# Weights of the first norm as one row, spread by a product with ones; new order of the first transfers; dt of batch 0 in four tiles

## The reference

```python
h = rmsnorm(hidden_states, ln1_w)            # x * rsqrt(mean(x*x) + eps) * ln1_w
zxbcdt = h @ w_in.T                          # 512 -> 512 + 768 + 4 columns
z, xs, Bs, Cs, dt = jnp.split(zxbcdt, ...)
xBC = silu(conv(concat([xs, Bs, Cs])) + conv_b)
dt = softplus(dt + dt_bias); A = -exp(A_log)
... # chunked scan over 4 chunks of 128 positions, gate with silu(z), @ w_out.T
```

## Time and profile before

| | |
|---|---|
| median of 3 runs | 495.55 us (494.87 to 496.28) |
| the profiled execution | 494.94 us, its span 493.2 us |
| TensorE busy | 473.5 us, 96% of the span |
| VectorE, ScalarE, GpSimd busy | 316.8, 236.8, 215.1 us |
| mean granted clock of TensorE | 0.994 |
| TensorE's share of the chain that ended last | 80% |

### The profile page before, as it was taken

How to read it: one execution, slowest core, us unless ns; L and a number is a source line. 1 busy time by engine, 2 the same in 40 slices (tenths; PEclk the granted TensorE clock), 3 DMA queues, 4 the chain that set the end, 5 groups by cost and what they waited for, 6 DMA issues and landing times.

```text
span 493.2 us, 6223 instructions
## 1 busy us (share of the span) xinstructions
PE 473.5 (96%) x2104; PEld 377.1 (76%) x2104; DVE 316.8 (64%) x518; ACT 236.8 (48%) x444; POOL 215.1 (44%) x242
## 2 busy tenths in 40 slices
PE   8998999988999989999999899999999999999995
PEld 7886677765767768888788778888888888888884
DVE  3793587746688856677998889865957523411223
ACT  5887667766556666455343245234805430033300
POOL 5835476526773596767877000010004442133321
PEclk9998999999999999999999999999999999999998
DMA  7531022003212415342332166410300000200001
GB/s 247 200 110 49 38 86 65 21 23 102 75 59 86 167 45 193 130 171 86 130 105 83 69 214 213 170 45 7 122 21 1 0 0 1 85 2 0 2 15 70
DMA packets 14431, 40.80 MB, mean 83 GB/s; under 512 B 2368, under 2 KB 2368, under 8 KB 14400
## 3 DMA queue, kind: packets, MB, share of 16 engines
q1 hardware_dynamic: 14400, 40.41, 24.1%
HBM read 38.30 MB, written 2.10 MB: 82 GB/s over the span
## 4 chain that ended last, share of the span: by engine, by line
PE 80%; DVE 11%; issue 4%; ACT 3%; POOL 2%; POOLq 0%; DVEq 0%
PE psA L1621 8%; PE psA L1622 8%; PE psA L1410 6%; PE psA L1412 6%; PE psB L1631 4%; PE psB L1630 4%; PE psA L1416 3%; PE psA L1418 3%; PE psA L1600 3%; PE psA L1599 3%; PE psA L1596 3%; DVE xbc L1168 3%; PE psB L1596 2%; PE psB L1600 2%; PE psB L1599 2%
## 5 line engine op out<-in xcount | busy, mean ns | idle before, releaser
L1621 PE MATMUL psA<-xT_h,q_gu 128*128 128x512 f32 x176 | 70.1, 398 | 0.0
L1622 PE MATMUL psA<-xT_l,q_gu 128*128 128x512 f32 x176 | 69.1, 393 | 0.0
L669 POOL TENSOR_SCALAR var<-mv 128x1 f32<-128x1 f32 x16 | 4.9, 305 | 128.7 <-DVE mv L1060 128.6
L1031 ACT ACTIVATE gate_t<-psA 128x512 f32<-128x512 f32 x22 | 13.2, 598 | 75.1 <-PE psA L1622 75.1
L816 POOL TENSOR_TENSOR int_l<-prod_t,int_h 128x512 fp32r<-128x512 f32 x22 | 28.7, 1306 | 45.7 <-ACT int_h L1036 45.7
L1362 DVE TENSOR_TENSOR prod_t<-gate_t,psA 128x512 f32<-128x512 f32 x22 | 15.1, 689 | 51.7 <-PE psA L1622 48.6
L727 POOL TENSOR_TENSOR beta<-wsum,beta 128x512 fp32r<-128x512 f32 x28 | 36.1, 1312 | 24.8 <-ACT beta L892 24.8
L1621 PEld LDWEIGHTS psA<-xT_h,q_gu 128*128 128x128 f32 x176 | 33.1, 188 | 8.2
L1622 PEld LDWEIGHTS psA<-xT_l,q_gu 128*128 128x128 f32 x176 | 33.1, 188 | 7.4
L1631 PE MATMUL psB<-q_dn,int_l 128*128 128x512 f32 x88 | 34.3, 389 | 0.0
L1630 PE MATMUL psB<-q_dn,int_h 128*128 128x512 f32 x88 | 34.2, 389 | 0.0
(11 more groups left out here) (251 smaller groups left out, 1358.8 us busy)
## 6 DMA issues: line engine op xcount, KB each, us to landing
raw<-in_f_gu_t SPq DMA_DIRECT2D x22, 512.0 KB, 3.3
raw<-in_w_gu_t SPq DMA_DIRECT2D x14, 512.0 KB, 3.8
raw<-in_f_dn_t SPq DMA_DIRECT2D x10, 512.0 KB, 3.6
raw<-in_w_gu_t SPq DMA_DIRECT2D x14, 256.0 KB, 2.9
raw<-in_w_dn_t SPq DMA_DIRECT2D x7, 512.0 KB, 3.3
raw<-in_w_in_t SPq DMA_DIRECT2D x5, 512.0 KB, 4.4
x<-in_hidden SPq DMA_DIRECT2D x8, 256.0 KB, 4.9
out<-x SPq DMA_DIRECT2D x8, 256.0 KB, 2.0
```

The costliest lines, as they stand in the source:

```text
L1621: nc.tensor.matmul(ps, w, seq(xT_h, k, b), start=k == 0, stop=False)
L1622: done = nc.tensor.matmul(ps, w, seq(xT_l, k, b), start=False, stop=k == KD - 1)
```

## The change

The weights of the first norm come as one row of 512 (2 KB) and not as 128 copies (256 KB). A product of a row of ones with this row spreads them over the 128 partitions of a bank of `psA`, and VectorE copies them to `ln1_sb`. TensorE's thirty transposes of the identity become 8 ahead of this product and 18 behind it. On SyncE's queue the row goes first, the four tiles of batch 0 follow, the weights of dt have a semaphore of their own, and the first input weights go ahead of five small constants. dt of batch 0 is made for one tile of 128 positions at a time, and `aneg` moves on ScalarE from `prepare` to behind the copy of dt.

```diff
-    steps += [("norm1", t) for t in range(NC)]
+    steps += [("ln1rows",)] + [("norm1", t) for t in range(NC)]
     steps += [("turn1", 0), ("turn1", 1), ("prepare",), ("turn1", 2), ("turn1", 3), load("in", 0)]
+    steps += [("dtpart", c) for c in range(NC - 1)]
     steps += [("norm1", 4), ("norm1", 5), ("dt", 0), load("in", 1), ("norm1", 6), ("norm1", 7)]
...
-WARM_UP = 30
+WARM_FIRST, WARM_UP = 8, 18
 KEEP_WARM = {1: 11, 2: 8, 3: 9}
...
-            load_x(0)
-            load_x(1)
-            sp.dma_start(ln1_sb[:], ln1_w.to_broadcast([P, D])).then_inc(ln1_loaded, 16)
-            for t in range(2, NC):
+            sp.dma_start(ln1_row[:], ln1_w).then_inc(ln1_loaded, 16)
+            for t in range(NC):
                 load_x(t)
-
-            sp.dma_start(wdt_raw[:], w_dt).then_inc(consts_loaded, 16)
+            sp.dma_start(wdt_raw[:], w_dt).then_inc(wdt_loaded, 16)
+            load_weights(0)
             sp.dma_start(alog_sb[:], a_log.to_broadcast([P, H])).then_inc(consts_loaded, 16)
...
+            nc.gpsimd.memset(one_row[:], 1.0)
...
-                s.wait_ge(consts_loaded, N_CONST)
+                s.wait_ge(wdt_loaded, 16)
                 s.wait_ge(wdt_ready, 1)
                 nc.scalar.activation(wdt[:, :, 0:H], wdt_raw[:], ACT.Copy).then_inc(wdt_ready, 1)
-                nc.scalar.activation(aneg[:], alog_sb[:], ACT.Exp).then_inc(aexp_ready, 1)
...
+                    if b == 0:
+                        s.wait_ge(consts_loaded, N_CONST)
+                        nc.scalar.activation(aneg[:], alog_sb[:], ACT.Exp).then_inc(aexp_ready, 1)
...
+                if kind == "ln1rows":
+                    v.wait_ge(*done_a(step))
+                    nc.vector.tensor_copy(ln1_sb[:], bank_a(step)).then_inc(freed_a(step)[0], 1)
+                elif kind == "norm1":
...
                     if t == 0:
-                        v.wait_ge(ln1_loaded, 16)
+                        v.wait_ge(*freed_a(("ln1rows",)))
...
+            def part_of_dt(c):
+
+                pe.wait_ge(xTh_ready, TURNS.index(("turn1", c)) + 1)
+                pe.wait_ge(wdt_ready, 3)
+                ps = open_a(("dt", 0)) if c == 0 else bank_a(("dt", 0))
+                for k in range(KD):
+                    nc.tensor.matmul(ps[:, chunk(c)], wdt[:, k, :], xT_h[:, k, chunk(c)], start=c == 0 and k == 0,
+                                     stop=False)
+                pe.wait_ge(*freed_b(("turn1", c)))
+                for k in range(KD):
+                    done = nc.tensor.matmul(ps[:, chunk(c)], wdt[:, k, :], xT_l[:, k, chunk(c)], start=False,
+                                            stop=c == NC - 1 and k == KD - 1)
+                return done
+
+            keep_warm(WARM_FIRST)
...
+                if kind == "ln1rows":
+
+                    pe.wait_ge(ln1_loaded, 16)
+                    nc.tensor.matmul(open_a(step), one_row[:], ln1_row[:], start=True, stop=True).then_inc(a_done, 1)
+                    keep_warm(WARM_UP)
+                elif kind == "dtpart":
+                    part_of_dt(at[0])
...
+                elif step == ("dt", 0):
+                    part_of_dt(NC - 1).then_inc(a_done, 1)
```

More of the change, by code:

```diff
@@ L270, in psum_jobs @@
         kind, at = s[0], s[1:]
-        if kind == "dt":
-            a.append(("dt", *at))
+        if kind == "ln1rows" or kind == "dt" and at[0] == 1:
+            a.append(s)
+        elif kind == "dtpart" and at[0] == 0:
+            a.append(("dt", 0))
         elif kind == "inproj":
@@ L374, in layer_kernel @@
             ("t_f", 134912, [P, 4, 2, P], F32), ("ln2_sb", 140032, [P, D], F32), ("nrm2", 142080, [P, D], F32))
-        xn, ln1_sb, wdt = overlay(("xn", 61440, [P, NT, D], F32), ("ln1_sb", 77824, [P, D], F32),
-                                  ("wdt", 79872, [P, KD, P], F32R))
+        xn, ln1_sb, wdt, ln1_row, one_row = overlay(("xn", 61440, [P, NT, D], F32), ("ln1_sb", 77824, [P, D], F32),
+                                           ("wdt", 79872, [P, KD, P], F32R), ("ln1_row", 81920, [1, D], F32),
+                                           ("one_row", 83968, [1, P], F32))
         tT_h, tT_l, alpha, act, beta, a22, wsum, u_t, v_t, c12, q8 = overlay(
@@ L402, in layer_kernel @@
         ln2_loaded = sem("ln2_loaded")
+        wdt_loaded = sem("wdt_loaded")
         consts_loaded = sem("consts_loaded")
@@ L583, in layer_kernel @@
         NORMS = [s for s in SCHEDULE if s[0] in ("norm1", "outproj", "ln1", "ln2")]
-        N_CONST = 16 * 6
+        N_CONST = 16 * 5
         def norm_number(step):
@@ L625, in _, with load_weights @@
             sources = {"in": w_in, "out": w_out, "ga": w_gu, "gb": w_gu, "dn": w_dn, "sumgu": f_gu, "qgu": f_gu, "sumdn": f_dn, "qdn": f_dn}
-            load_x(0)
-            load_x(1)
-            sp.dma_start(ln1_sb[:], ln1_w.to_broadcast([P, D])).then_inc(ln1_loaded, 16)
-            for t in range(2, NC):
+            def load_weights(n):
+                kind, *at = LOADS[n]
+                src = sources[kind][at[0]]
+                wide = down_width(at[0]) if kind in ("sumdn", "qdn") else KD * P if kind == "ga" else RAW
+                sp.dma_start(raw[:, n % RAW_SLOTS, 0:wide], src[:, 0:wide]).then_inc(raw_loaded[n % RAW_SLOTS], 16)
+            sp.dma_start(ln1_row[:], ln1_w).then_inc(ln1_loaded, 16)
+            for t in range(NC):
                 load_x(t)
-            sp.dma_start(wdt_raw[:], w_dt).then_inc(consts_loaded, 16)
+            sp.dma_start(wdt_raw[:], w_dt).then_inc(wdt_loaded, 16)
+            load_weights(0)
             sp.dma_start(alog_sb[:], a_log.to_broadcast([P, H])).then_inc(consts_loaded, 16)
@@ L637, in _ @@
             sp.dma_start(convb_sb[:], conv_b).then_inc(consts_loaded, 16)
-            for n, (kind, *at) in enumerate(LOADS):
+            for n in range(len(LOADS)):
                 if n >= RAW_SLOTS:
@@ L642, in _ @@
                         sp.wait_ge(*used)
-                src = sources[kind][at[0]]
-                wide = down_width(at[0]) if kind in ("sumdn", "qdn") else KD * P if kind == "ga" else RAW
-                sp.dma_start(raw[:, n % RAW_SLOTS, 0:wide], src[:, 0:wide]).then_inc(raw_loaded[n % RAW_SLOTS], 16)
+                if n >= 1:
+                    load_weights(n)
                 if n == 1:
@@ L689, in prepare @@
             def prepare():
-                pool.wait_ge(consts_loaded, N_CONST)
+                pool.wait_ge(wdt_loaded, 16)
                 pool.wait_ge(wdt_ready, 2)
@@ L695, in prepare @@
                     .then_inc(wdt_ready, 1)
+                pool.wait_ge(consts_loaded, N_CONST)
                 nc.gpsimd.tensor_tensor(heads(diag_d[:]), ident[:].unsqueeze(1).to_broadcast([P, H, P]),
@@ L1063, in _ @@
                 kind, at = step[0], step[1:]
-                if kind == "norm1":
+                if kind == "ln1rows":
+                    v.wait_ge(*done_a(step))
+                    nc.vector.tensor_copy(ln1_sb[:], bank_a(step)).then_inc(freed_a(step)[0], 1)
+                elif kind == "norm1":
                     t = at[0]
@@ L1446, in keep_warm @@
                     nc.tensor.transpose(psA[:, 3, 0:P], ident[:], ident[:])
-            keep_warm(WARM_UP)
+            def part_of_dt(c):
[11 more added lines that the diff above has]
+            keep_warm(WARM_FIRST)
             for step in SCHEDULE:
                 kind, at = step[0], step[1:]
-                if kind == "turn1":
+                if kind == "ln1rows":
[4 more added lines that the diff above has]
+                    part_of_dt(at[0])
+                elif kind == "turn1":
                     pe.wait_ge(nrm_ready, at[0] + 1)
```

## The result

The changed kernel takes **498.43 us** (median of 4 runs, 497.74 to 498.88); the kernel before, beside it on the same chip, 495.21 us (494.73 to 496.28). The ratio is 1.006, with an interval from 1.0046 to 1.0075: about 3 us slower, near the forecast of 498.5. The profiled execution took 497.74 us.

The account below looks back on a forecast made before the run. Past the start TensorE bounds the kernel; the first 45 us hang on dt, norms, VectorE's convolutions and ScalarE. 0.44 + 7.10 + 0.15 - 2.32 - 0.7 - 1.7 = +3.0, giving 498.5 us; range 494.8 to 500.4, the forecast's own 497.6 to 500.4.

Parts of the forecast that it names:

- That is 0.44 us later than 7.31: TensorE's start: eight fillers, the product with ones and 18 fillers end at 7.75, so the first tile's transpose starts 0.44 later.
- The remark under the rivals: TensorE's start: a clock rise one or two us later, from the one-row product, would add up to 1 us.
- I take 0.222: dt in four tiles: each of 32 narrow fp32r products costs 0.222 us, 7.10 in all.
- rival 2: dt: not slower, a narrow product costs one pass, 0.111; 495.0 with the clock held, 496.6 without; chance 0.31.
- 0.7 is given back: Between the copy of dt and the last norm: VectorE is free sooner, so the norm starts 4.7 us later, not 5.37.
- The gap and the clock: Ahead of the scan: TensorE's idle gap shrinks from 1.95 to 1.2 us and the clock behind it stays at 1.00.
- I take the 1.7 us as given back: Behind the scan's start: the held clock returns the 1.7 us lost to half clock over 3.4 us.
- The dt term: dt of batch 0 in tiles: 7.10 us for 32 products, where weight load to copy took 2.32 before.
- the clock's credit: Behind the gap ahead of the scan: 1.7 us subtracted in the sum because the clock holds.

Follow-up runs that it names:

- the row later: Changed kernel with 18 fillers ahead of the product with ones and 6 behind, not 8 and 18: 498.94 us against 495.23 for the kernel before, 1.0074.

## Why the prediction was right in time and wrong in parts

By its own steps, changed kernel against its terms:

1. **"That is 0.44 us later than 7.31" failed**: it was 2.55, which is 2.1 more. Counted from weight load to weight load, as the prediction does: the memset of `one_row`, taken as nothing, delays the first filler by 0.13 (2.42 to 2.55). The eight fillers took 1.89 (to 4.44) and not 1.74, the product 2.01 (to 6.45) and not 1.72. A slip of 0.08 is in the sum itself, since 4.16 + 1.72 is 5.88 and not 5.8. The large piece is the eighteen fillers behind the product, 3.41 (to 9.86) and not 1.96, as TensorE reached its full pace at 9.64 and not at 5.7. The remark under the rivals, a rise one or two us later because of the one row, named the product that the experiments point at, and foresaw about half of the delay (full pace from 9.64 and not 5.89). That the product is a cause is shown: on one row in place of all rows it costs 1.7 us. How it does so is open, and so is how much of this pair's 2.55 is chance: in the six traces that begin with thirty fillers the first transpose lies between 7.31 and 8.58, 8.0 in the mean, and the prediction's 7.31 is the earliest of them.
2. **"I take 0.222" failed**: a narrow product costs 0.111, the pace of one pass in L1531, so 3.6 us in place of 7.10. This was rival 2's price and the widest term. The Trainium skill, TensorE: Matmul & The Clock Gate, section Back-to-back issue gap, has about 81 ns for a weight load with its product over 128 columns. The trace's 0.111 us stands above it; by the skill's figure, as an estimate, the term would be 2.6.
3. **"0.7 is given back" held**: the last norm stands 5.07 us behind the copy of dt, and 5.81 before, 0.74 less. It still took 2.87, as forecast.
4. **The gap and the clock held, but not their worth.** The gap was 1.1 us where 1.2 was forecast and the clock 1.00, and 1.55 us came back at 53.44. The step **"I take the 1.7 us as given back" failed** behind that point. Two small VectorE operations beside GpSimd's products took 1.58 us more than before, TensorE then waited 0.9 us for `state`, and 0.43 us was left (3.22 less 2.79). The kernel with the gap filled shows the same collision without the change, and 0.4 us. The Trainium skill, SBUF — State Buffer, section SBUF: two separate sides, says that VectorE and GpSimd share one pair of ports, that a VectorE operation with two SBUF inputs (against a GpSimd operation that reads SBUF) or in a two-port mode needs it, and that whichever starts first holds it for its whole instruction while the other blocks. L1147 has two such inputs, and its 0.17 and 0.96 us agree; in which mode L1149 ran no run shows. The length of the gap does not decide about the clock behind it: in four of the experiments a gap of 2.0 or 2.1 us ahead of the scan left it at 1.00.

In sum: 2.55 at the start, 1.43 more up to the copy of dt (3.98), 0.74 given back, 0.02 more given back on the way to the scan (3.22), and 0.43 given back behind its start. That makes 2.79, against a forecast of 3.0. The dt term was 3.5 us too high, the start 2.1 too low, and the clock's credit 1.3 too high, so that the errors nearly cancel (3.5 - 2.1 - 1.3 = 0.1). So the time came right by luck: the forecast put the loss in the tiles of dt, and the run without them loses 2.9 us all the same.

The part that was to help did nothing, since TensorE and not the weights' arrival held the first tile back, as the prediction said.

What stays open: what in the product with part of the rows delays the rise, and what decides where it comes when there is no such product; why the kernel with the row on all rows is still 0.9 to 1.5 us slower than before (the tiles of dt, 0.5 by their median, the 2.00 us product where fillers stood, and the later transfer would fill it, but this is argued and was not run apart).

## What to carry to other kernels

Price a narrow product by the pace of its nearest like, record by record, not by the call; and give each term its own check, since a total can be right by two errors. While the clock is still low, TensorE's fillers are not free room: a product on one row put between them cost 1.7 us more than one on all rows. Where a VectorE operation on the chain takes four to six times its usual time, look at what GpSimd does beside it: here one wait that let a norm of 0.75 us go first gained 1.8 us.

## What the runs showed of the hardware that was not expected

- The moment at which TensorE doubles its pace differs between executions of the same start, while the granted clock reads full all along. With thirty fillers from 2.4 us the weight loads are 0.109 apart from 5.89 (before), 6.06, 7.12, 8.00, 8.44 and 8.58 on. With a product on all rows among them it is 5.98 and 8.38 (the same kernel) and 7.31. With a product on 64 rows behind the first eight it is 8.85, and on one row 9.64 (the change), 10.16 and 10.92. One profiled execution does not fix this term to better than about 1.3 us at the first transpose.
- The stretch of low clock moves too: 46.90 to 50.30 before, between 174 and 182 in seven experiments, 10.3 to 13.7 with the row later.
- Behind fillers on 128 rows, the weight load of a product on 1 or 64 rows has a standstill of 0.33 us ahead of it; that of one on 128 rows has none.
- Narrowing an fp32r product from 512 to 128 columns takes its pace from 0.23 to 0.111 us, a half and not a quarter.
- A VectorE operation on 128x16 elements takes 0.96 us beside a GpSimd product of 1.04, and 0.17 alone.
